# Gathers of expert results: four a quad instead of three, started one quad behind the batch's last page

## The reference

```
x = x + cross_attention(layernorm(x), context)        # 16 heads of 8
x = x + moe(layernorm(x))
moe(h): shared = silu(h @ sg.T) * (h @ su.T) @ sd.T    # every token
        scores = sigmoid(h @ gate.T) + bias            # 64 experts in 8 groups
        keep the 4 best groups, then the 6 best experts of a token; weights / their sum
        routed = sum over the 6 of weight * (silu(h @ eg.T) * (h @ eu.T)) @ ed.T
        return shared + routed
```

## Time and profile before

| | us |
|---|---|
| three timed runs | 592.63, 593.04, 596.70 |
| median | 593.04 |
| span of the profiled execution | 792.4 |

### The profile page before, as it was taken

The page is one execution under the profiler, slowest core; times in us unless marked ns, Lnnn a source line. Parts: engine busy times, 40 slices in busy tenths (PEclk is TensorE's granted clock), DMA queues, the critical chain, the costliest instruction groups (busy, mean ns, idle before and its releaser), DMA issues.

```text
span 792.4 us, 12061 instructions
## 1 busy us (share of the span) xinstructions
PE 503.3 (64%) x3204; PEld 420.8 (53%) x3204; DVE 456.1 (58%) x2264; ACT 352.3 (44%) x962; POOL 389.3 (49%) x425
## 2 busy tenths in 40 slices
PE   3767555766555574632359956788688889777700
PEld 2445334444334343311359856778688789777700
DVE  6587556667555576656233624576776756346532
ACT  3564433344443343322215934466666766246400
POOL 2006445654455655556650055454554545555574
PEclk9885555555555555555568976899988876897555
DMA  7532123322123332223425533455455555654421
GB/s 195 194 113 94 62 100 107 104 100 98 47 80 107 107 100 98 95 78 129 124 81 134 148 94 95 106 138 151 126 145 137 151 137 146 160 153 107 113 70 47
DMA packets 98708, 90.60 MB, mean 114 GB/s; under 512 B 10576, under 2 KB 85456, under 8 KB 98640
## 3 DMA queue, kind: packets, MB, share of 16 engines
q1 hardware_dynamic: 85232, 64.26, 27.5%
q0 software_dynamic: 12288, 25.29, 11.3%
q10 hardware_dynamic: 1120, 0.28, 0.2%
HBM read 41.32 MB, written 48.46 MB: 113 GB/s over the span
## 4 chain that ended last, share of the span: by engine, by line
PE 30%; another core or an unknown queue 17%; issue 16%; ACT 14%; POOL 11%; DVE 9%; ACTq 2%; DMA 0%; POOLq 0%; DVEq 0%
PE bank_s L1155 14%; POOL pages L447 6%; PE bank_o L1155 4%; PE bank_q L1155 3%; PE bank_s L1151 2%; ACT d_now L511 2%; ACT p_t L533 2%; ACT pxt L511 2%; POOL empty L492 2%; ACT gu_now L511 2%; ACT k_exp L521 1%; ACT s_act L672 1%; POOL p_t L492 1%; PE bank_o L1151 1%
## 5 line engine op out<-in xcount | busy, mean ns | idle before, releaser
L1155 PE MATMUL bank_s<-pxt,gu_now 128*128 128x64 f32 x768 | 116.5, 316 | 51.6 <-ACT pxt L511 31.3
L492 POOL DMA_INDIRECT p_t<-results,place_i x96 | 91.1, 949 | 110.6 <-ACT s_act L672 72.8
L1155 PEld LDWEIGHTS bank_s<-pxt,gu_now 128*128 128x128 f32 x768 | 111.4, 231 | 58.1 <-ACT pxt L511 36.4
L492 POOL DMA_INDIRECT empty<-results,place_i x96 | 91.1, 949 | 77.2 <-issue 35.1
L1111 DVE TENSOR_TENSOR h_t<-bank_s,s_act 64x256 f32<-64x256 f32 x128 | 54.7, 427 | 113.9 <-ACT s_act L672 95.4
L447 POOL DMA_INDIRECT pages<-payload,place_i x96 | 93.0, 968 | 37.9 <-issue 27.0
L447 POOL DMA_INDIRECT pages<-payload_b,place_i x96 | 92.8, 967 | 35.8 <-issue 26.7
L437 POOL TENSOR_TENSOR rstd<-ve,minus_half 128x4 f32<-128x4 f32 (+1 forms) x21 | 18.6, 885 | 132.6 <-DVE ve L927 130.0
L672 ACT ACTIVATE s_act<-bank_s 64x512 f32<-64x512 f32 x64 | 37.8, 590 | 79.5 <-remote 36.0
L533 ACT ACTIVATE p_t<-bank_s 128x512 f32<-128x512 f32 x64 | 36.2, 598 | 67.9 <-issue 27.9
L1255 PE MATMUL bank_o<-bias_h,row_h 96*128 96x256 bf16 x16 | 6.1, 381 | 72.2 <-ACT o_t L511 70.3
(11 more groups left out here) (169 smaller groups left out, 1164.1 us busy)
## 6 DMA issues: line engine op xcount, KB each, us to landing
pg<-pages SPq DMA_DIRECT2D x64, 258.0 KB
results<-y_s SPq DMA_DIRECT2D x64, 256.0 KB
pages<-empty SPq DMA_DIRECT2D x21, 774.0 KB
w_gu<-in_expert_gu SPq DMA_DIRECT2D x16, 256.0 KB
w_d<-in_expert_d SPq DMA_DIRECT2D x31, 128.0 KB
out_x<-xb SPq DMA_DIRECT2D x16, 128.0 KB
xb<-in_x SPq DMA_DIRECT2D x3, 512.0 KB, 8.0
pages<-payload,place_i POOLq DMA_INDIRECT x96
```

Of the source, the lines that this page charges most:

```text
L492: pool.indirect_dma_start(out=ys[n % YS_SLOTS][:, k, :], out_offset=None, in_=results[0:landed * QUAD * P, :], in_offset=bass.IndirectOffs ...
L1155: return pe.matmul(dst, w, v, start=True, stop=True)
```

## The change

- A batch's twelve gathers start at quad `gathers_from[b]`: one quad behind the one that completes the batch, 12 + 3b for batches 0 to 13, then 62 and 65. Four DMAs are issued a quad, each on an event of its own: the silu, then the next quad's `pxt`, then `h_t`, then the copy of `y_s`.
- The two sums of a batch stand at quads `gathers_from[b] + 3` and `+ 4`: two sums in three quads. Gathers of batch 14 start in quad 62, those of batch 15 run behind the quads: 16 gathers in all.
- `pages` and `results` become two tensors each, for the first 200 pages and the last 56; the places of batches 14 and 15 count from zero again. The number of fills stays 22; the first has eight pages instead of four.
- `quad_at`, `landed_before` and `turn_of` allow for another order of quads and batches.
- The output of batch i is stored at SyncE's step 24 + 3i instead of 25 + 4i.

```diff
-FIRST_STORE = FIRST_SUM + 2 * TPB + STORE_BEHIND
-GATHERS_A_QUAD = TOPK // 2
-FIRST_BEAT = FIRST_SUM - 6
+GATHERS_A_QUAD = 4
+FRESH_AT = NQ - (E // HALVES + 2 * FILL) // QUAD
+FRESH_QUADS = NQ - SPLIT_QUAD
...
+        def quad_at(p):
+
+            if p < FRESH_AT:
+                return p
+            return p - FRESH_AT + SPLIT_QUAD if p < FRESH_AT + FRESH_QUADS else p - FRESH_QUADS
+
+        def landed_before(b):
+
+            n = quads_before(b)
+            if b >= SPLIT:
+                return n - SPLIT_QUAD + FRESH_AT
+            return n if n <= FRESH_AT else n + FRESH_QUADS
+
+        turn_of = sorted(range(B), key=landed_before)
+        gathers_from = []
+        for b in turn_of:
+            gathers_from.append(max(landed_before(b) + 1, gathers_from[-1] + TPB * TOPK // GATHERS_A_QUAD if gathers_from else 0))
+
+        def summed_at(p):
+
+            return [TPB * i + t for i in range(B) for t in range(TPB) if gathers_from[i] + 3 + t == p]
...
-                if q == FIRST_STORE + 2 * TPB * stored:
+                if q == gathers_from[stored] + 4 + STORE_BEHIND + 2:
                     store(stored)
...
-            def beat(step):
+            def beat(i, step):
 
                 q, part = divmod(step, GATHERS_A_QUAD)
+                q += gathers_from[i]
+                if q >= NQ:
+                    return
                 if part == 0:
                     pool.wait_ge(act_ready, q + 1)
                 elif part == 1:
+                    pool.wait_ge(pxt_ready, min(q + 2, NQ))
+                elif part == 2:
                     pool.wait_ge(h_ready, HALVES * (q + 1))
                 else:
                     pool.wait_ge(y_ready, q)
...
                 for k in range(TOPK):
-                    if GATHERS_A_QUAD * FIRST_BEAT + TOPK * n + k < GATHERS_A_QUAD * NQ:
-                        beat(GATHERS_A_QUAD * FIRST_BEAT + TOPK * n + k)
-                    pool.indirect_dma_start(out=ys[n % YS_SLOTS][:, k, :], out_offset=None, in_=results[0:landed * QUAD * P, :],
-                                            in_offset=bass.IndirectOffsetOnAxis(ap=place_i[:, n, k:k + 1], axis=0)
+                    beat(i, t * TOPK + k)
+                    pool.indirect_dma_start(out=ys[n % YS_SLOTS][:, k, :], out_offset=None, in_=done,
+                                            in_offset=bass.IndirectOffsetOnAxis(ap=place_i[:, tile, k:k + 1], axis=0)
                                             ).then_inc(ys_in[n % YS_SLOTS], 16)
...
             def combine_next(q):
-                n, odd = divmod(q - FIRST_SUM, 2)
-                if n >= 0 and not odd:
+                for n in summed_at(q):
                     combine(n)
```

More of the change, by code:

```diff
@@ L81, with build @@
 POWER_AFTER = {}
-def build(nc, x, ctx_cols, wq, bq, wk, bk, wv, bv, wo, bo, gate_cols, gate_bias, expert_gu, expert_d, shared_gu, shared_d, out, pages, results):
+def build(nc, x, ctx_cols, wq, bq, wk, bk, wv, bv, wo, bo, gate_cols, gate_bias, expert_gu, expert_d, shared_gu, shared_d, out, old_pages, new_pages, old_results, new_results):
     with ExitStack() as ctx:
@@ L255, in build @@
         out_v = out.rearrange("b (t p) h -> p (b t) h", p=P)
-        fill_v = pages[FIRST_FILL * P:PAGES * P, :].rearrange("(k p r) c -> k p (r c)", p=P, r=FILL)
-        quad_v = pages.rearrange("(q g p) c -> q p g c", g=QUAD, p=P)
-        results_v = results.rearrange("(q g p) h -> q p g h", g=QUAD, p=P)
+        pages_v = [pages.rearrange("(q g p) c -> q p g c", g=QUAD, p=P) for pages in (old_pages, new_pages)]
+        results_v = [results.rearrange("(q g p) h -> q p g h", g=QUAD, p=P) for results in (old_results, new_results)]
         def line(ap):
@@ L272, in quads_before, with quad_in, held @@
             return pages_before(b) // QUAD
-        def fills_before(b):
-            return 1 + (pages_before(b) - FIRST_FILL + FILL - 1) // FILL
-        def held(q):
+        def quad_at(p):
[13 more added lines that the diff above has]
+            return [TPB * i + t for i in range(B) for t in range(TPB) if gathers_from[i] + 3 + t == p]
+        def fills_before(b):
+            if b < SPLIT:
+                return 1 + (pages_before(b) - OLD_PAGES % FILL + FILL - 1) // FILL
+            return OLD_FILLS + 1 + (pages_before(b) - OLD_PAGES - NEW_PAGES % FILL + FILL - 1) // FILL
+        def quad_in(both, p):
+            q = quad_at(p)
+            new = q >= SPLIT_QUAD
+            at = q - SPLIT_QUAD if new else q
+            return both[new][at:at + 1, :, :, :]
+        def held(p):
+            q = quad_at(p)
             for start in (0, SPLIT_QUAD):
@@ L381, in _ @@
                     pages_complete(SPLIT)
-                if q == SPLIT_QUAD:
+                if q == FRESH_AT:
                     pages_complete(B)
@@ L446, in scatter @@
                 for k in range(first, after):
-                    pool.indirect_dma_start(out=pages[:, :], out_offset=bass.IndirectOffsetOnAxis(
+                    pool.indirect_dma_start(out=(new_pages if n >= SPLIT else old_pages)[:, :], out_offset=bass.IndirectOffsetOnAxis(
                         ap=place_i[:, TPB * n + t, k:k + 1], axis=0), in_=payload[n % 2][:, t, k, :],
@@ L481, in gather @@
             def gather(n):
-                landed = quads_before(n // TPB)
-                if n % TPB == 0:
+                i, t = divmod(n, TPB)
+                b = turn_of[i]
+                tile = TPB * b + t
+                done = (new_results[0:(quads_before(b) - SPLIT_QUAD) * QUAD * P, :] if b >= SPLIT
+                        else old_results[0:quads_before(b) * QUAD * P, :])
+                landed = landed_before(turn_of[i])
+                if t == 0:
                     for j in range(SLOTS):
@@ L1142, in _ @@
                 quad(q)
-            for n in range((NQ - FIRST_SUM + 1) // 2, TPB * B):
-                combine(n)
+            for n in range(TPB * B):
+                if gathers_from[n // TPB] + 3 + n % TPB >= NQ:
+                    combine(n)
         @block.tensor
@@ L1412 @@
     args.append(nc.dram_tensor("out_x", (B, TOK, D), F32, kind="ExternalOutput").ap())
-    args.append(nc.dram_tensor("pages", (PAGES * P, PC), F32, kind="Internal").ap())
-    args.append(nc.dram_tensor("results", (PAGES * P, D), F32, kind="Internal").ap())
+    args += [nc.dram_tensor(f"{age}_pages", (n * P, PC), F32, kind="Internal").ap() for age, n in (("old", OLD_PAGES), ("new", NEW_PAGES))]
+    args += [nc.dram_tensor(f"{age}_results", (n * P, D), F32, kind="Internal").ap() for age, n in (("old", OLD_PAGES), ("new", NEW_PAGES))]
     build(nc, *args)
```

49 lines of the change are left out of this document (29 added, 20 removed).

## The result

| | median us | runs | lowest to highest |
|---|---|---|---|
| before | 593.56 | 4 | 592.63 to 596.7 |
| after | 622.57 | 4 | 617.82 to 626.95 |

The ratio is 1.048, with a 95% interval of 1.041 to 1.055: the change costs 29 us. The forecast was 611, in a range up to 622; the side is right, the time is 11.6 us longer than foretold, and the median lies 0.6 us above the range.

What follows compares the result with a forecast made beforehand. GpSimd's queue was taken as the bound. Before's shortest way, 587.8 us, plus 25.9 us of idle GpSimd gave 613.7; about 2.7 given back made 611 us, range 582 to 622.

Steps and rivals of the forecast that it cites:

- The late signals: Signals arriving late beside GpSimd's DMAs in the 792.4 us profile; claimed to hardly exist in timed runs.
- GpSimd's queue is the bound: From first scatter to last gather GpSimd's queue sets the time: 16.2 us a scatter batch, 1.25 us a gather.
- The shortest way of before: Sum for the kernel before without late signals, from first scatter at 60.7 to the final store: 587.8 us.
- the 5.2 us: Rest between 587.8 and before's 593.04 median; placed in the quads, where after hides it behind GpSimd.
- Four a quad, paced by GpSimd: Quads 12 to 53: twelve gathers per three quads take 15.0 us, so GpSimd sets 5.0 us a quad.
- The gap: GpSimd idle 25.9 us after batch 13's last gather, until silu 62 lets batch 14's gathers start.
- its silu 0.6 earlier: After batch 13's last sum: quad 56's product at 553.9, its silu at 553.3, then six quads of 3.48 us.
- rival C: Quads 12 to 53: TensorE's waits halve its clock, 34 us more if half run so, 645 us; chance 0.07.
- Give back about 2.7 us: Taken off 613.7 because TensorE and ScalarE stand a quad ahead when VectorE comes free, giving 611 us.
- The tail: From silu 62: 24 gathers, 30.0 us, plus 8.2 to the end; 16 gathers behind the last quad's.
- A: Rival: timed quads already take 5.0 us or more, so four gathers fit; faster, about 582 us; chance 0.25.
- B: Rival: the 0.30 us between gathers belongs to the recording, a gather steps by 0.95; no change, 590 us; chance 0.18.

Runs made afterwards that it cites:

- before again: The kernel before, unchanged, profiled a second time: 597.06 us measured, profile span 595.2.
- five gathers a tile: The kernel before without each tile's sixth gather and its term of the sum (sixth expert's share missing from the output): 574.77 us, ratio 0.9653.
- eleven tight batches: The kernel after, but only the first eleven batches have their sums in three quads, later ones in four: 612.21 us, ratio 1.0294 to before.
- sums two later: The kernel after with both sums of each batch two quads later and nothing else: 618.2 us, ratio 1.0380 to before.
- the packing moved: The kernel after with VectorE's packing of a quad's expert numbers put ahead of the previous quad's sum, not behind: 622.69 us, ratio 1.0474 to before.

## Why the prediction was half right

**The late signals.** Right. The profile before was 792.4 us by its recording; the same kernel gave 595.2 in a second one. The step of 1.25 us, read in the disturbed trace, holds in all of the others.

**GpSimd's queue is the bound.** Right for the gathers, by before again (240.4 us without a hole) and by the table, with only about 20 us to spare before the quads bind instead (five gathers a tile). "From the first scatter" is more than the runs bear out: the scatters do run without a hole (292.5 - 65.11 = 227.4 us for 14 batches, 226.8 foretold), but with one batch of them less ahead of the first load the first quad came no earlier. The shortest way of before was summed to 587.8 and 5.2 us were left over. They lie ahead of the gathers: in before again the first scatter starts at 65.11, not 60.73, and the first gather at 345.77, not 339.6. From gather 1 to the end the sum had 248.2, and it is 249.4. The 6.2 us more ahead of gather 1 (345.77 - 339.6), term by term: the first scatter 4.4 later, the 14 batches 0.6 longer, from their end to silu 0 11.7 us where the estimate had 9, and the twelve quads behind it 40.2 instead of 41.8.

```profile
65.11 1.19 POOL L447 DMA_INDIRECT pages<-payload,place_i  x1 [10.86 <-DVE place_i L886]
```

**Where to put the 5.2 us.** This is the first term that failed. The prediction saw both cases, "if in the attention stage, after is 618.9; if in the quads, after hides them", and took the quads, because VectorE's sum of 4.1 us a quad fitted. The number is near the 3.91 measured, but that was luck: VectorE was busy for 145.88 of the 171.90 us of before again, 3.3 a quad (the groups of the earlier trace rows overlap, and product and copies from 544.23 to 546.48 are 2.25 us, not the 2.47 added up), while TensorE was busy for 160.04, 3.6 a quad, and was no term of that sum. And GpSimd was gapless over these quads, so nothing could be hidden there. Gather 1 is at 345.6 instead of 339.6 in after, 6 us of what is missing. In the two profiles in which the first scatter came earlier (first gathers at 340.7 and 340.8) the front was that of the sum, so its length varies by 5 us from execution to execution.

**Memories, order, store, start of the gathers: 0.** Right: ratio 1.0015 with the memories alone, and the first gather is released by silu 12 in both.

**Four a quad, paced by GpSimd.** The mechanism is right and its size is close. Twelve gathers per three quads measure 15.1 us; the quads up to silu 56 average 4.77, since they had a lead at first and fell back on GpSimd's pace by sum after sum that waited (21.3 us in 8 places on one buffer name, 8.9 in 5 on the other). Batch 13's last gather, predicted to be through at 549.6, was through at 556.7, late by the front and by 1 us from steps of 1.257 instead of 1.25.

**The gap.** It is where foretold, between the 168th and the 169th gather, and ends with silu 62. Predicted 25.9 us, measured 28.7. The terms: from the end of batch 13's steps (556.7) its landing and VectorE's start took 2.0 instead of 1.65; the sum took 2.3 as predicted. But then the term "its silu 0.6 earlier" was wrong. Silu 56 had been out at 553.9, 4.8 us before the sum began, and the next one, of quad 57, stood behind the packing and ScalarE's copies, 2.6 us after the sum. From there five quads, not six, at 4.07 instead of 3.48: 20.4 against 20.9. And 1.4 to the gather. 2.0 + 2.3 + 2.6 + 20.4 + 1.4 = 28.7.

**Quads 54 to 61 near 3.5 us.** Wrong. The prediction had 3.48 from a stretch at full clock. The five quads of the gap took 4.07 on average at a clock of 0.81 in after:

```profile
563.60:584.00 20.40, 19.28 (x136) 18.41 (x136) 11.12 (x58) 17.25 (x56) 0.00 (x0) 0.81 0.30 85
```

The average hides two kinds of quad. The first two took 4.84 and 5.04 us, the other three 3.43, 3.54 and 3.52, which is the prediction's number. The stretches of the first and the third (length, busy PE, PEld, DVE, ACT, POOL, granted clock, DMA share, GB/s), and TensorE's order of time up to the first and in the third:

```profile
563.60:568.50 4.90, 4.36 (x21) 4.06 (x21) 2.25 (x12) 3.40 (x13) 0.00 (x0) 0.50 0.21 59
573.50:577.00 3.50, 3.23 (x29) 3.04 (x29) 2.25 (x12) 3.40 (x13) 0.00 (x0) 1.00 0.39 112
```

```profile
562.15 2.08 PE L1204 MATMUL bank_o<-w_d,h_t 128*128 128x128 f32 x8 [4.69 <-DVE h_t L1159]
564.77 3.68 PE L1204 MATMUL bank_s<-pxt,gu_now 128*128 128x64 f32 x16 [0.54 <-ACT pxt L559]
...
574.65 2.00 PE L1204 MATMUL bank_s<-pxt,gu_now 128*128 128x64 f32 x16 [0.27 <-ACT pxt L559]
```

TensorE had stood for 4.69 us for the product behind the waiting sum, and came out of it at half clock: the same sixteen matmuls take 3.68 us at 0.50 and 2.00 at 1.00. A quad wholly at 0.50 took 5.87 us (eleven tight batches, sums two later), less than the 6.6 us that rival C took for TensorE's work alone. With the packing moved the five took 3.55 at 1.00, and with eleven tight batches four took 4.6 at 0.73. So rival C's mechanism was there, at the one place where it counts: 3 us in after (4.84 + 5.04 less twice 3.48). The reading that C gave for it was not right, though: the 5s of the clock row lie ahead of 396 us and behind 732, and its slices of 19.8 us between them show 6 to 9, so that row can't tell what a single wait does. Ahead of it the clock fell as well (0.90 from silu 12 to 56 against 1.00), and cost nothing that these rows show, since the quads waited for GpSimd anyhow.

**"Give back about 2.7 us."** Wrong as a separate term. The quad of lead was real (silu 56 out before the sum, so five quads and not six), 3.5 us, but packing and copies (2.6) and the clock (2.9) took more than that back. Without it the prediction's sum was 613.7, and the terms above bring it to the measured span: 613.7 + 6.0 (front) + 1.1 (steps) + 2.8 (gap) - 0.3 (tail) = 623.3. So of the 12.3 us from 611 to the profile's span 6.0 are the front, 1.1 the steps, 2.8 the gap and 2.7 this term, less 0.3 of the tail. The front is no part of what the change does: before has it too, and there it was the 5.2 us left over.

**The tail.** Right: 16 gathers behind the last quad's, 24 from silu 62, and gather 169 to the end in 37.9 us (predicted 38.2). From the last silu (587.2) to the end it is 36.1 us (about 34 foretold; 47.0 in the first recording of before and 53.2 in before again).

**The rivals.** A is excluded by quads of 3.91 us in before again. B is excluded by the step of 1.26 in the profiles of before again and after, whose spans lie within 0.2% of the medians. The 645 that the sum would give if a gather paid for VectorE's copies is excluded as well: the step is 1.257 with four gathers a quad and 1.258 with three. The Trainium skill, page SBUF — State Buffer, section Who interferes with whom, says that VectorE's two-port copies shut GpSimd out while they run; no trace here shows it in the step of an indirect DMA.

**What stays open.** With the packing moved, the gap shrank by 4.4 us in the profile and the median did not move. Four runs of after spread over 9 us, with a front that varies by 5, so a difference of this size is not settled. No edit changes the clock alone; that it makes these quads long rests on the same matmuls at both clocks within one stretch, and on the quads of four profiles. Open too is what sets the 3.9 us of a quad in before, where TensorE is busy for 93% of the time and VectorE for 85%.

## What to carry to other kernels

Ask for the pace of the queue before asking for more of it in each turn: four gathers a quad cannot be had from an engine that does three in a quad. With the sums four quads behind, the gathers just fall back and nothing is lost; with the sums right behind, what gives way is the quad. A consumer placed right behind its producer turns the producer's pace into the pace of everything that is queued behind the consumer. That can be free for long, while the producer is the bound anyhow, and is paid at the first point at which the producer needs something that the slowed side makes: find that point, and count how much of the other side's work is still ahead of it there. Where it is only the last dependence, half of the change costs nearly nothing (4 us of 28 here), so a share for each turn is the wrong rule.

## What the hardware showed that was not expected

- One recording of a kernel was off by 200 us: 792.4 against 595.2 for the same program, with signals up to 13 us late beside GpSimd's DMAs in the first. Durations and steps of instructions were the same in both (0.94 us a gather, 1.25 from one to the next), and they were enough to rebuild the timed run to about 1%.
- GpSimd's step was the steadiest number of the case: 209.5 to 210.5 us for 167 steps in eleven profiles, beside quads of 3.9 to 4.8 us and a DMA rate of 171 to 193 GB/s.
- TensorE's granted clock was 1.00 in 344 to 516 us of before again, and 0.90 from 344 to 554 us of after, where TensorE pauses at each sum that waits; the same number of matmuls had it busy for 160.0 and 179.3 us.
- Half the granted clock did not double a quad: 3.5 us at 1.00, 4.84 to 5.87 at 0.50, where the sixteen gate and up matmuls of a quad went from 2.00 to 3.68 us.
